# A new table of places for a two-phase Trainium2 kernel: applied-inverse sets one to a step, the inverse over four steps, its transposes behind the step of the key products, state inputs stored a step later

## The chip, the cores and the metric

The kernel runs on one core of one Trainium2 chip. The metric is the device time of one execution in microseconds. Times are given as the median of several runs.

## What is computed

The input x is (8, 1024, 256), float32: 8 sequences of the outer index, 1024 rows (tokens for the attention part, batch rows for the gated part), 256 features. Three residual layers follow each other:

```python
x = x + 0.5 * ffn(layernorm(x), ...)
x = x + attn(layernorm(x), ...)
x = x + 0.5 * ffn(layernorm(x), ...)      # the same weights as the first
```

`ffn` is a gated recurrence over the outer index (8 steps), for each row by itself:

```python
ft = sigmoid(xt @ wf.T + c @ uf.T + bf)
it = sigmoid(xt @ wi.T + c @ ui.T + bi)
gt = tanh(xt @ wc.T + c @ uc.T + bc)
c  = ft * c + it * gt
...
h = tanh(einsum('tbi,oi->tbo', x, wo) + c_final @ uo.T + bo)
```

`attn` has 16 heads of width 16. Its keys k are also its queries (a root-mean-square norm of the input by head), v is minus the static output x @ W.T, and a gated delta rule runs along the 1024 tokens:

```python
S = S * lam
err = v_t - einsum('bhk,bhkv->bhv', k_t, S)
S = S + beta * (k_t[..., :, None] * err[..., None, :])
o_t = einsum('bhk,bhkv->bhv', q_t, S)
...
return layernorm(static_out + o)
```

## The kernel before

**Blocks and steps.** The 1024 rows are cut into 8 blocks of 128. The first gated layer (`ff`) takes a block through 8 steps (one per outer index), then the second gated layer (`fg`) does the same: 16 blocks of 8 steps, numbered b = 0 to 15, i = 8b + t. A step of the gated layer is 24 weight products of 128x128 on TensorE (12 with the layer's input, 12 with the state c, `pe_step`, L471; the trace has two records for each), sigmoids and a tanh on ScalarE (L488, L495), and a product and a sum on VectorE (L515, L517) that give the next c. The end of L517 is called the cell below.

**The attention part.** The delta rule is done in chunks of 16 tokens. For a chunk a 16x16 triangular matrix is inverted, and then 64 hops (`hop_at`, two for each of 32 pieces) carry the state S along the tokens. A block n of 128 tokens passes through these named pieces:

- preparation (`prep_pe`, `prep_act`, `prep_dve`, `prep_pool`): `ln2_late` and `lc2` (statistics L83 and coefficients L89 to L95 of the layer norm), `apply` on GpSimd, `lt0`, `lt1` (transposes of the normed rows, L696), `square`, `sums` (L624), `rms` (11 operations, L57 to L65 on 128x128), `key` (L635), `keys` (L642 on VectorE, L681 on GpSimd), `v01`, `v23` (the static products, L706, copied by ScalarE at L761), `kt0`, `kt1` (transposes of the keys, L715), `km0`, `km1` (masked copies, L655, L772), `g0` to `g3` (products of keys with keys, L735; read by ScalarE at L784 and then by VectorE at L661);
- the solve (`solve_pe`, `solve_act`, `solve_dve`): `gt0`, `gt1` (transposes, L870, and the table product L805), `inv1` to `inv3` (the inversion level by level on VectorE, L821 and L824), `al`, `tt0`, `tt1` (transposes of the inverse, L882, evicted at L832 by VectorE and L853 by ScalarE), and `ta0` to `ta7` (the sets that apply the inverse to keys and values, L899; even ones are evicted by ScalarE at L860, odd ones by VectorE at L839, into `xs_out`).

The inversion has 14 levels m = 14 to 1, two operations each; L788 says which levels a piece has, and the elements of an operation are 8 x m x (15 - m):

```python
INV = {"inv1": range(C - 2, 10, -1), "inv2": range(10, 4, -1), "inv3": range(4, 0, -1)}
```

**Where a piece stands.** `PERIOD` (L159) has for each step t four lists, and `CLOSE` (L167) four lists for the end of a block. An entry (2, "tt0") at step t means: in step t of block b, do tt0 of block b - 2. Every engine walks the same table, so a place in it sets the order on TensorE, ScalarE, VectorE and GpSimd at once. `fill_table` (L197) follows it to know which use of a PSUM bank comes after which: transposes, v and al take banks 4 and 5 in turn, the g products banks 6 and 7, and set ta m bank 6 + m % 2. `refill` (L363) waits until the bank's last use has been read.

**First phase** (`first_pe`, `first_dve`, L967 to L1020, blocks 0 to 5): no hops. TensorE does half of the input products, list 0, the other half, list 1, half of the state products, list 2, the other half, list 3. VectorE and ScalarE do lists 0 to 2 before the cell and list 3 behind it.

**Second phase** (`second_pe` L1228, `second_dve` L1309, i = 48 on): hop s runs at i = 49 + s. In a step TensorE does the hop's state products (`hop_states_pe`, L1093), 8 state products of the gates, the hop's update (`hop_update_pe`, L1110), the other 4, and then four times a quarter of the next step's input products followed by one of the four lists. VectorE does in a step, in this order: zbd from the update (`state_dve`, L1134), fcig and the cell, the late normalisation (`post_dve`, L1167, L83 to L95), and all four lists. The hop's update is written to banks 4 and 5 too: `refill` for a piece in these banks waits until zbd has been read out of them on both VectorE and ScalarE (L1127), and the update waits until all pieces before it have been read. Hops and preparation overlap in blocks 6 to 9; the late normalisation runs from block 7 on.

**Transfers** go through SyncE's queue in the order of the code (`first_sp`, `second_sp`, `transfers` at L947): x1 to memory, the next x, alpha, `xs_out` in two halves (`store_xs`, L940, 512 KB twice; the eviction of the next half's sets waits for the landing), kg; in the second phase also the loads of xs and kg for hop s + 2 and the stores of e.

## Time and profile before

| | us |
|---|---|
| median of 3 runs | 1365.33 |
| lowest and highest | 1364.75 and 1370.57 |
| the profiled execution | 1362.08 |
| its span | 1360.3 |
| mean granted TensorE clock in it | 0.982 |

The span runs from the first to the last instruction of the program; the execution's own time is 1.8 us longer. The granted clock is a share of full speed: 1.00 is 2.4 GHz, 0.50 is 1.2 GHz. Busy times count each engine by itself. PE is TensorE's products, PEld its weight loads, DVE VectorE, ACT ScalarE, POOL GpSimd, SP SyncE. A timeline's row gives the start in us from the span's start, the length, the operation, and in brackets how long the engine was idle before it and what ended that; "issue" is a wait for which the profile shows no cause. A row of busy times by stretch has its start and end, its length, the busy time of PE, PEld, DVE, ACT and POOL with the records of each, the mean granted clock, the DMA engines' busy share and their GB/s.

### The profile page before, as it was taken

The numbers are of one execution on the slowest core, as the hardware profiler recorded it, in microseconds if no ns is written. First come the engines' busy times: TensorE is split into PE (matmuls) and PEld (weight loads), VectorE is DVE, ScalarE is ACT, GpSimd is POOL, SyncE is SP. The second block draws the span as 40 slices with busy tenths as digits, with TensorE's granted clock in tenths as the row PEclk, the third lists the DMA queues.
The fourth block names the chain that finished last, engine by engine and source line by source line (L and its number), as shares of the span: only waits on it lengthen the run. The fifth ranks groups of instructions, "written<-read, shape, count | busy, mean of one in ns | idle before, by whom it ended". The sixth has DMA issues, their size and how long they took to land.

```text
span 1360.3 us, 57987 instructions
## 1 busy us (share of the span) xinstructions
PE 1261.8 (93%) x25763; PEld 1167.5 (86%) x25763; DVE 856.1 (63%) x2047; ACT 665.3 (49%) x1623; POOL 273.3 (20%) x350
## 2 busy tenths in 40 slices
PE   6999999999999999898898889899999999999997
PEld 6989998989989888787778887888889989898886
DVE  4556886868778676567657764854445646354622
ACT  3344444454444545453564556356455756655432
POOL 0113112031221211112502230230230405050500
PEclk9999999999999999998899999899999999999999
DMA  4010101122121222242225213323324242333000
GB/s 147 1 63 32 66 33 67 65 79 65 52 80 51 103 70 90 69 129 71 69 65 166 66 54 112 109 83 108 117 91 147 66 134 82 110 102 109 1 32 31
DMA packets 72425, 108.35 MB, mean 80 GB/s; under 512 B 12400, under 2 KB 49520, under 8 KB 70128
## 3 DMA queue, kind: packets, MB, share of 16 engines
q1 hardware_dynamic: 72176, 104.65, 24.0%
q8 instruction: 203, 3.33, 1.0%
q14 instruction: 46, 0.38, 0.1%
HBM read 53.74 MB, written 50.86 MB: 77 GB/s over the span
## 4 chain that ended last, share of the span: by engine, by line
PE 75%; DVE 12%; ACT 7%; issue 5%; DMA 0%; SPq 0%; DVEq 0%; ACTq 0%
PE ps L471 41%; PE ps L543 7%; PE ps L899 6%; PE ps L1093 5%; PE ps L1110 4%; PE ps L706 3%; ACT gates L488 3%; ACT zbd L1127 2%; PE ps L431 2%; DVE ln_bn L83 2%; PE ps L735 1%; DVE hs L557 1%; PE ps L870 1%; PE ps L696 1%; DVE ffn_rows L568 1%
## 5 line engine op out<-in xcount | busy, mean ns | idle before, releaser
L471 PE MATMUL ps<-gates,wt 128*128 128x128 f32 x2688 | 350.5, 283 | 2.9 <-DVE gates L517 2.9
L471 PEld LDWEIGHTS ps<-gates,wt 128*128 128x128 f32 x2688 | 320.9, 195 | 14.0 <-DVE gates L517 3.6
L471 PE MATMUL ps<-ffn_rows,wt 128*128 128x128 f32 x2304 | 296.7, 281 | 10.1 <-DVE hs L557 3.7
L471 PEld LDWEIGHTS ps<-ffn_rows,wt 128*128 128x128 f32 x2304 | 276.6, 195 | 20.1 <-issue 12.5
L488 ACT ACTIVATE gates<-ps,colv 128x128 f32<-128x128 f32 x448 | 127.6, 369 | 194.8 <-PE ps L471 194.5
L515 DVE TENSOR_TENSOR fcig<-gates 128x512 f32<-128x512 f32 x112 | 83.9, 750 | 163.5 <-ACT gates L495 129.8
L1134 DVE TENSOR_TENSOR zbd<-ps,mask 64x1024 f32<-64x1024 f32 x63 | 76.5, 1214 | 127.9 <-PE ps L1110 127.9
L1196 POOL TENSOR_TENSOR ffn_rows<-ffn_rows,rowv 128x256 f32<-128x256 f32 x64 | 53.9, 878 | 347.0 <-DMA ffn_rows<-x_scratch 347.0
L1127 ACT ACTIVATE zbd<-ps,mask 32x256 f32<-32x256 f32 x252 | 103.8, 458 | 9.9 <-PE ps L1110 6.9
L899 PE MATMUL ps<-inv_cols,kv 32*32 32x32 f32 x8192 | 88.3, 194 | 15.8 <-issue 13.7
L899 PEld LDWEIGHTS ps<-inv_cols,kv 32*32 32x32 f32 x8192 | 79.1, 104 | 27.7 <-issue 18.7
L471 PE MATMUL ps<-kg_rows,wt 128*128 128x128 f32 x768 | 95.1, 278 | 6.5 <-DVE hs_more L557 3.5
L471 PEld LDWEIGHTS ps<-kg_rows,wt 128*128 128x128 f32 x768 | 89.2, 192 | 10.3 <-issue 5.8
L543 PE MATMUL ps<-wt,ffn_rows 128*128 128x256 f32 x384 | 91.8, 384 | 5.8 <-DVE hs L557 3.0
L1119 ACT COPY e<-ps 128x512 f32<-128x512 f32 x64 | 37.4, 584 | 116.2 <-PE ps L1093 116.1
L122 POOL TENSOR_SCALAR key_rows<-ffn_rows,ln_stats 128x256 f32<-128x256 f32 x64 | 40.2, 643 | 256.4 <-PE ps L870 168.1
L1093 PE MATMUL ps<-zbd,xsb 128*32 128x64 f32 x4096 | 84.1, 235 | 6.7 <-issue 6.7
L1093 PEld LDWEIGHTS ps<-zbd,xsb 128*32 128x32 f32 x4096 | 73.8, 148 | 18.0 <-issue 12.7
L543 PEld LDWEIGHTS ps<-wt,ffn_rows 128*128 128x128 f32 x384 | 70.0, 190 | 17.4 <-ACT gates L488 4.1
L681 POOL TENSOR_TENSOR kg_rows<-key_rows,g_tok 128x512 f32<-128x512 f32 x32 | 47.6, 1519 | 185.8 <-DVE key_rows L635 185.8
L83 DVE BATCH_NORM_STATS2 ln_bn<-ffn_rows 128x6 f32<-128x256 f32 x248 | 83.9, 410 | 0.5
L1110 PE MATMUL ps<-e,kgb 32*64 32x64 f32 x4032 | 74.3, 221 | 2.1 <-issue 1.1
(127 smaller groups left out, 1726.8 us busy)
## 6 DMA issues: line engine op xcount, KB each, us to landing
xs_scratch<-xs_out SPq DMA_DIRECT2D x32, 512.0 KB, 3.5
xsb<-xs_scratch SPq DMA_DIRECT2D x256, 64.0 KB
ffn_rows<-x SPq DMA_DIRECT2D x32, 256.0 KB, 3.4
x_scratch<-ffn_rows SPq DMA_DIRECT2D x32, 256.0 KB, 2.7
kg_scratch<-kg_rows SPq DMA_DIRECT2D x32, 256.0 KB, 2.8
kgb<-kg_scratch SPq DMA_DIRECT2D x256, 32.0 KB, 2.3
e_scratch<-e SPq DMA_DIRECT2D x256, 32.0 KB, 1.7
ffn_rows<-e_scratch SPq DMA_DIRECT2D x8, 1024.0 KB
```

Source lines behind the costliest of these rows:

```text
L83: link(dve.bn_stats(stats[:, b, 0:6], src[:, b, :]))
L471: mm = pe.matmul(banks[g][:, col:col + P], wt[:, w, k, m * P:(m + 1) * P], rhs, start=(x in (0, FI)), stop=(k == KT - 1 and (t == 0 or x > ...
L488: a = act.activation(gates[q][:, g, m * P:(m + 1) * P], fi[:, g * D + m * P:g * D + (m + 1) * P], ACT.Sigmoid, bias=bias[:, g, m:m + 1])
L515: dve.tensor_tensor(fcig, gates[q][:, 0:2, :], gates[q][:, 2:4, :], ALU.mult).then_inc(self.products, 2)
L543: mm = pe.matmul(h_b[j][:, e * D:(e + 1) * D], self.xnT[b.n % len(self.xnT)][:, k, 2 * j + e, :], wt[:, WO, k, :], start=(e == 0 and k == ...
L681: pool.tensor_tensor(kg_rows.rearrange("p (b h d) -> p b h d", h=H, d=HD)[:, 2 * r:2 * r + 2, :, :], key_rows.rearrange("p (b h d) -> p b ...
L899: mm = pe.matmul(dst.ps[32 * c:32 * c + 32, 32 * k:32 * k + 32], kv_of(n)[tok, lane, :], invT[tok, lane, :], start=True, stop=True, skip_g ...
L1093: mm = pe.matmul(E_BANK[32 * g:32 * g + 32, 64 * kk:64 * kk + 64], xs_cols[:, k // C, k % C, C * a:C * a + 2 * C], zbd[:, k, :], start=Tru ...
L1110: mm = pe.matmul(S_BANKS[out_rows, k % C, :], kgb[32 * g:32 * g + 32, a, 64 * kk:64 * kk + 64], es[a][32 * g:32 * g + 32, 64 * kk:64 * kk ...
L1127: act.activation(zbd[rows, C:2 * C, cols], S_BANKS[rows, :, cols], ACT.Copy, scale=mask4[rows, c:c + 1]).then_inc(z_done, 1)
L1134: dve.tensor_tensor(zbd[0:64, 0:C, :].rearrange("p k (c d) -> p k c d", c=SETS), S_BANKS[0:64, :, :].rearrange("p k (c d) -> p k c d", c=S ...
L1196: pool.tensor_tensor(xt[p][:, r, :], xt[p][:, r, :], rowv[:, 2, :], ALU.add).then_inc(post_done, 1)
```

## The change

Only numbers of the table, one split of the inversion and one line of the transfers change. By step: set ta m of a block moves so that steps 0 to 6 hold ta2, ta3, ta4, ta5, ta6 and ta7, ta0, ta1 (before: ta4; ta5 and ta6; ta7; none in step 4; ta0 and ta1; ta2; ta3 in `CLOSE`). `inv2` is cut in two (levels 10 to 8 in step 2, 7 to 5 in step 3) and the last levels, now `inv4`, move from step 3 to step 4. `v01` moves from step 3 to step 4, list 1; `v23` to the end of step 4. `sums` moves to step 3, `rms` to the end of step 4, `tt0` and `tt1` to step 5, `key` and `keys` behind them. The first half of `xs_out` is stored in step 1 in place of step 0, and behind the stores of x1.

```diff
@@ -156,15 +156,15 @@
-PERIOD = {0: ([], [(2, "g3abcd")], [], [(1, "ln2_late")]),
...
-          4: ([(1, "v23"), (1, "sums")], [(1, "rms")], [(2, "tt0")], [(2, "tt1"), (1, "key")]),
...
+PERIOD = {0: ([], [(2, "g3abcd")], [], [(1, "ln2_late"), (3, "ta2abcd")]),
...
+          4: ([(3, "ta6abcd"), (2, "inv4")], [(1, "v01")], [(3, "ta7abcd")], [(1, "v23"), (1, "rms")]),
...
-CLOSE = ([], [(2, "ta3abcd")], [], [(1, "g2abcd")])
+CLOSE = ([], [], [], [(1, "g2abcd")])
@@ -785,7 +785,7 @@
-        INV = {"inv1": range(C - 2, 10, -1), "inv2": range(10, 4, -1), "inv3": range(4, 0, -1)}
+        INV = {"inv1": range(C - 2, 10, -1), "inv2": range(10, 7, -1), "inv3": range(7, 4, -1), "inv4": range(4, 0, -1)}
@@ -947,10 +947,10 @@
-            if t in (0, 4) and stored.real:
-                store_xs(sp, stored, t // 4)
             if t in (0, 1) and prep.real:
                 store_x1(sp, prep, (2 * t, 2 * t + 1))
+            if t in (1, 4) and stored.real:
+                store_xs(sp, stored, t // 4)
```

On VectorE, block 7, the end of step 2's pieces (L821 and L824 are the two operations of a level, with the elements of each) and what follows them; before:

```order
L821 TENSOR_TENSOR prod<-inv 128x448
L824 TENSOR_TENSOR inv<-inv,prod 128x8x8x7
L821 TENSOR_TENSOR prod<-inv 128x448
L824 TENSOR_TENSOR inv<-inv,prod 128x8x7x8
L821 TENSOR_TENSOR prod<-inv 128x432
L824 TENSOR_TENSOR inv<-inv,prod 128x8x6x9
L821 TENSOR_TENSOR prod<-inv 128x400
L824 TENSOR_TENSOR inv<-inv,prod 128x8x5x10
L1134 TENSOR_TENSOR zbd<-ps,mask 64x1024
L515 TENSOR_TENSOR fcig<-gates 128x512
```

And now:

```order
L821 TENSOR_TENSOR prod<-inv 128x448
L824 TENSOR_TENSOR inv<-inv,prod 128x8x8x7
L1134 TENSOR_TENSOR zbd<-ps,mask 64x1024
L515 TENSOR_TENSOR fcig<-gates 128x512
L517 TENSOR_TENSOR gates<-fcig 128x256
L89 BN_AGGR ln_bn<-ln_bn 128x2 x8
```

Levels 7, 6 and 5 no longer stand ahead of zbd, fcig and the cell; they come after the late normalisation's coefficients of the next step.

On VectorE, block 7, from the last operation of rms on; before, in step 4:

```order
L65 SCALAR_TENSOR_TENSOR rms<-hs,rms 128x128
L832 TENSOR_SCALAR inv_cols<-ps,mask 128x128x4 x4
L635 TENSOR_TENSOR key_rows<-key_rows,rms 128x2048
L1134 TENSOR_TENSOR zbd<-ps,mask 64x1024
L515 TENSOR_TENSOR fcig<-gates 128x512
L517 TENSOR_TENSOR gates<-fcig 128x256
L642 TENSOR_TENSOR kv<-key_rows,lam_tok 128x128x16
```

And now, in steps 4 and 5:

```order
L65 SCALAR_TENSOR_TENSOR rms<-hs,rms 128x128
L1134 TENSOR_TENSOR zbd<-ps,mask 64x1024
L515 TENSOR_TENSOR fcig<-gates 128x512
L517 TENSOR_TENSOR gates<-fcig 128x256
L832 TENSOR_SCALAR inv_cols<-ps,mask 128x128x4 x4
L635 TENSOR_TENSOR key_rows<-key_rows,rms 128x2048
L642 TENSOR_TENSOR kv<-key_rows,lam_tok 128x128x16
```

The evictions of the transposed inverse (L832) and key (L635) moved behind the cell, so rms is no longer right ahead of them.

On TensorE, block 7, steps 4 and 5; before:

```order
L471 MATMUL ps<-ffn_rows,wt 128x128 x3
L706 MATMUL ps<-wt,key_cols 128x256 x8
L471 MATMUL ps<-ffn_rows,wt 128x128 x6
L882 MATMUL ps<-ident,inv 128x128 x8
L471 MATMUL ps<-ffn_rows,wt 128x128 x3
L882 MATMUL ps<-ident,inv 128x128 x8
L1093 MATMUL ps<-zbd,xsb 32x64 x32
L471 MATMUL ps<-gates,wt 128x128 x8
L1110 MATMUL ps<-e,kgb 64x64 x32
L471 MATMUL ps<-gates,wt 128x128 x4
```

And now step 4:

```order
L471 MATMUL ps<-ffn_rows,wt 128x128 x3
L899 MATMUL ps<-inv_cols,kv 32x32 x64
L471 MATMUL ps<-ffn_rows,wt 128x128 x3
L706 MATMUL ps<-wt,key_cols 128x256 x8
L471 MATMUL ps<-ffn_rows,wt 128x128 x3
L899 MATMUL ps<-inv_cols,kv 32x32 x64
L471 MATMUL ps<-ffn_rows,wt 128x128 x3
L706 MATMUL ps<-wt,key_cols 128x256 x8
L1093 MATMUL ps<-zbd,xsb 32x64 x32
```

Step 4 holds two sets and both halves of v in place of one half of v and the transposes; the transposes follow in step 5.

## Rows read from the trace of the kernel before

**Rows 1.** The page, engines: busy us (share of the span) xinstructions.

```profile
PE 1261.8 (93%) x25763; PEld 1167.5 (86%) x25763; DVE 856.1 (63%) x2047; ACT 665.3 (49%) x1623; POOL 273.3 (20%) x350
```

**Rows 2.** By stretch: its length, busy us (records) of PE, PEld, DVE, ACT, POOL; clock, DMA.

```profile
24.00:478.60 454.60, 438.08 (x7812) 412.35 (x7810) 335.40 (x858) 204.51 (x497) 86.49 (x108) 1.00 0.16 57
478.60:925.10 446.50, 403.33 (x10613) 365.29 (x10602) 300.09 (x651) 227.00 (x521) 93.95 (x116) 0.95 0.29 88
```

**Rows 3.** The same by interval: block 7 (1 to 5), block 9, one without pieces.

```profile
602.50:615.60 13.10, 13.10 (x518) 12.38 (x518) 12.09 (x38) 4.68 (x12) 4.71 (x8) 1.00 0.47 149
615.60:632.40 16.80, 12.31 (x239) 11.28 (x237) 16.35 (x29) 5.91 (x15) 7.42 (x8) 0.78 0.24 70
632.40:649.40 17.00, 16.83 (x335) 15.22 (x334) 9.23 (x33) 10.06 (x21) 1.05 (x2) 0.92 0.13 34
649.40:669.60 20.20, 16.44 (x343) 15.20 (x343) 15.45 (x21) 10.49 (x23) 17.00 (x19) 0.92 0.24 84
669.60:681.80 12.20, 11.13 (x318) 10.21 (x320) 5.32 (x6) 5.07 (x13) 0.00 (x0) 0.86 0.18 52
...
864.20:882.80 18.60, 14.47 (x438) 13.22 (x437) 18.15 (x27) 4.68 (x12) 8.46 (x8) 0.82 0.31 96
1190.90:1198.90 8.00, 8.00 (x180) 7.62 (x179) 7.24 (x15) 4.00 (x11) 0.00 (x0) 1.00 0.61 192
```

**Rows 4.** VectorE's timeline, block 7, interval 2.

```profile
621.09 0.73 DVE L839 TENSOR_SCALAR xs_out<-ps,w_x 128x512 f32<-128x512 f32 x1
...
626.39 0.62 DVE L821 TENSOR_TENSOR prod<-inv 128x448 f32<-128x448 f32 x1
...
630.09 1.21 DVE L1134 TENSOR_TENSOR zbd<-ps,mask 64x1024 f32<-64x1024 f32 x1
```

**Rows 5.** TensorE's waits, 478.6 to 1009.7 us: total, times, longest.

```profile
PE ps L899 <- issue: 13.7, 14, 3.1
PE ps L882 <- DVE inv_cols L832: 8.0, 3, 3.4
PE ps L1093 <- issue: 6.7, 5, 2.8
```

**Rows 6.** VectorE's timeline, block 7, steps 3 and 4.

```profile
635.98 0.75 DVE L839 TENSOR_SCALAR xs_out<-ps,w_x 128x512 f32<-128x512 f32 x1 [0.65 <-PE ps L899]
649.28 2.27 DVE L624 TENSOR_REDUCE rms<-key_half 128x128 f32<-128x2048 f32 x1
656.79 1.40 DVE L832 TENSOR_SCALAR inv_cols<-ps,mask 128x512 f32<-128x512 f32 x2
```

**Rows 7.** TensorE's timeline, blocks 7 to 9: the longest waits, and a half of v.

```profile
618.51 0.86 PE L899 MATMUL ps<-inv_cols,kv 32*32 32x32 f32 x48 [2.59 <-issue]
631.45 1.72 PE L696 MATMUL ps<-ident,key_rows 128*128 128x128 f32 x8 [1.91 <-DVE zbd L1134]
637.41 3.62 PE L706 MATMUL ps<-wt,key_cols 128*128 128x256 f32 x16
658.25 0.71 PE L882 MATMUL ps<-ident,inv 128*128 128x128 f32 x4 [3.40 <-DVE inv_cols L832]
871.51 1.51 PE L1093 MATMUL ps<-zbd,xsb 128*32 128x64 f32 x47 [2.83 <-issue]
```

**Rows 8.** The eleven stretches at half clock: one of them, and their sum.

```profile
631.70:635.10 3.40, 3.40 (x67) 3.17 (x69) 2.99 (x21) 2.48 (x3) 0.00 (x0) 0.50 0.09 30
...
sum 44.30, PE 42.88 PEld 39.58 DVE 28.43 ACT 11.94 POOL 24.15; mean PE 3.90 PEld 3.60 DVE 2.58 ACT 1.09 POOL 2.20
```

**Rows 9.** TensorE's waits in the first phase, 131 to 460 us.

```profile
PE ps L870 <- DVE key_rows L661: 5.7, 4, 1.4
...
PE ps L882 <- DVE inv_cols L832: 1.6, 1, 1.6
```

**Rows 10.** The page: the instruction queue, and a transfer's us to landing.

```profile
q8 instruction: 203, 3.33, 1.0%
...
xs_scratch<-xs_out SPq DMA_DIRECT2D x32, 512.0 KB, 3.5
```

10 rows, old and new, of the table PERIOD are left out of this document.

## The prediction

> **What bounds the kernel now.** I read the page's totals first, then busy times by stretch, then those of single steps, then TensorE's waits, then the timelines around the longest of them. The totals show TensorE busy for 93% of the span and VectorE for 63% [rows 1]. The change adds and removes no operation, so TensorE's 1261.8 us stay; it can only move idle time and time at half clock. By stretch [rows 2], the first phase is almost full from 24 to 478.6 us (438.08 of 454.60). From 478.6 to 925.1 us, where preparation and inverse run beside the state hops, it is busy 403.33 of 446.50 at a mean clock of 0.95. These 43 us of idle time are what the table can reach.
>
> Single intervals, from the end of one gate cell (L517) to the next, tell why. I call the one that follows the cell of step t "interval t"; VectorE does the pieces of step t in it. In block 7, VectorE is busy 12.09 of 13.10 in interval 1 and 16.35 of 16.80 in interval 2, while TensorE works 12.31 there; interval 2 of block 9 reads 18.15 of 18.60 [rows 3]. There VectorE is the bound: its zbd product (L1134), fcig and the cell stand behind all its pieces, from 630.09 to 632.4 [rows 4]. A step without pieces, the last row there, takes 8.00 with TensorE full [rows 3]. So an interval costs the larger of two sums: 8.0 plus TensorE's pieces, or VectorE's pieces plus about 2.5 for those three operations and their pauses.
>
> The other waits between 478.6 and 1009.7 us are 8.0 at the inverse's transposes (L882), which need a bank that VectorE empties only after rms, and 13.7 + 6.7 at L899 and L1093 for "issue", where the profile shows nothing that TensorE waits for [rows 5].
>
> **The inverse in four parts.** Three levels (m = 7, 6, 5) leave interval 2: six instructions, 626.39 to 630.09, 3.7 us. So does ta5's eviction (0.73), since the set left in step 2 is ta4, which ScalarE evicts [rows 4]. VectorE's pieces in intervals 1, 2 and 3 of blocks 7 and 8 become 11.4 (today's 13.1 less 2.5, plus 0.75 for ta3), 10.1 (5.5 of late normalisation from 615.6 to 621.09, and 4.6 for levels 10 to 8, between that eviction and 626.39), and 9.8 (3.0 to normalisation's coefficients, 632.4 to 635.4; sums 2.27; ta5 0.75; levels 7 to 5) [rows 3, 4, 6]. With 2.5 each this is a chain of 38.8, bound by VectorE. Interval 4 is led by TensorE: ta6, v01, ta7, v23 are 2 x 1.4 + 2 x 3.6 [rows 7], so 18.0, and 1.2 because GpSimd's work slows the cell's operations today and will again (an estimate). Sum 58.0. Today's four are 13.1 + 16.8 + 17.0 + 20.2 = 67.1, of which 3.4 is half clock on TensorE's own work (two stretches of 3.4 in intervals 3 and 4 [rows 8]): 63.7. Saving 5.7.
>
> What is late next: lt1's transposes use banks 4 and 5 and wait until VectorE has written zbd. Today they wait 1.91 [rows 7]. With ta6 no longer ahead of them I expect some 5 us of idle TensorE at that point. It lies inside the 38.8, but it shows that VectorE stays the bound for three steps.
>
> **The transposes a step later.** tt1's last four wait 3.40, because L832 stands behind sums and rms, from 649.28 to 656.79 [rows 6, 7]. In the change tt0 opens step 5, right behind the cell, and nothing is ahead of its eviction. That eviction (1.4 for a pair) still stands between tt0 and tt1's second fill, and the next one between tt1 and ta0: from the end of step 4's products that is 2.7 (to the cell's end, an estimate) + 1.4 + 0.7 + 1.4, some 6, where TensorE has about 4 us of its own work. So 2.0 are given back in step 5. key and keys (2.3 each) go to interval 5, where VectorE is busy 5.32 of 12.20 [rows 3]: hidden. **Blocks 7 and 8: -3.7 each.** Block 9 has no preparation left; its interval 2 loses the same 4.4 and interval 3 takes 1.4 of it back: **-3.** Block 6 has no late normalisation, the 5.5 that make VectorE the bound, and ln1 now stands behind key and keys: **-0.1.** Together -10.5.
>
> **First phase.** From block 2 on the largest waits are L870's 1.42 before gt0, once per block, and L882's 1.64, once [rows 9]. The latter goes: -1.6. ta2 now stands ahead of gt0 but needs g3's first bank, which VectorE frees only 0.4 before the second: 0.9 of waiting in place of 1.42, in blocks 3 to 5, -1.5. VectorE's load between two cells stays under TensorE's 11 (3.6 for v23, 2 for tt, 5.4 for the gates) in the worst step (rms, four evictions and key, 9.3, and the cell). **-3.** In the second phase ta2's bank costs 0.5 in four blocks, by the same reasoning; ta3's place between g1 and g2, whose banks it shares, becomes free, for which I take 0.75 a block: **-1.**
>
> **Stores.** The stores of xs_out go behind the x1 stores of step 1. SyncE then waits for ta3's eviction, about 5 us after the cell. Behind it stand the x1 load of blocks 7 and 8, which waits for GpSimd anyway, and the next e stores, which need the next hop. It lands 3.5 later [rows 10], ahead of ta4's eviction: 0. Without that cover ScalarE would hold the gates 1 to 3 us a block.
>
> **One set to a step.** One set is 128 products and 128 loads in 1.3 us. Of the 20.4 us of "issue", 9.8 lie in the VectorE-bound intervals (2.59 and 2.83 among them [rows 7]), 10.6 elsewhere. The longest cut a set in two where two sets stand close. The instruction queue moved 3.33 MB in 203 packets [rows 10]: 16.4 KB each, and 65 bytes for each of the 51,526 products and loads [rows 1], so a packet holds about one set. I read these waits as code that comes late. What spacing gives lies between 0 and -10.6; I take **-5**, as ta6 and ta7 still share step 4.
> The Trainium skill, "Runtime: NRT & Kernel Launch", Instruction fetch mechanics, has the same blocks of 256 instructions but calls their fetching hidden by the sequencer's pace. By it this term would be 0 and the sum 5 us higher; it speaks against what this part of the change can give.
>
> **The clock.** TensorE was granted half clock (1.2 in place of 2.4 GHz) for 44.3 us in eleven stretches, after idle time or after sets close together; 22 us at most hang on them. 17.1 us of the stretches lie in the VectorE-bound intervals, where they cost little; the rest costs up to 13.6 [rows 8]. The wait before lt1 should still bring the low level. Between 0 and -13.6; I take **-4.**
>
> **Sum.** -10.5 - 3 - 1 - 5 - 4 = -23.5 on the profiled execution of 1362.1: 1338.6. The median of the runs is 1365.3, 3.2 above it, so 1342.
>
> **Rivals.** (a) The chain moves and nothing else: neither code nor clock gains. 1365.3 - 14.5 = 1351. For it: the idle time before lt1 keeps the clock dips. Against it: sets that stop half way. It is also what the fetch rule of the Trainium skill's page gives, but for the clock.
> (b) VectorE only hands its load on. Its pieces still bind three steps, and step 4 holds 18 us of TensorE with v23 last, so that ScalarE's two copies of 0.6 and normalisation of 2.1 come ahead of the e copy: 2 to 3 more per block, and the clock dips grow with the 5 us of idle. The -14.5 shrinks to -3: 1362. For it: VectorE idles 5 us in today's interval 3, so the old table had room too. Against it: the 3.40 of L882 goes in any case.
> (c) Slower: key is late in every block. Counted from the end of step 4's products in the first phase, the cell, rms (3.6 to 4), four evictions (3.0), the pauses and key (2.3) end at about 12.2, and kt0 could start at 13.8. It decides from 1.6 us of lateness on: were key 5 us late, TensorE would idle 3.4 in each of 8 blocks, 27, less half of the gains above: +15, 1380. For it: today rms stands a step's half earlier. Against it: every term is a known duration.
>
> **How the numbers follow.** A measurement of this kernel tells about 0.5% (6.8 us) from no change. The forecast has 0.55 (1326 to 1350), (a) 0.20, (b) 0.14, (c) 0.08; 0.03 is for more than all terms at their best. At their best they are -14.5 - 10.6 - 13.6: 1326 or 1327. (b) gives 1362. Range 1326 to 1362. Faster by over 0.5% holds the forecast, (a) and the rest, 0.78; within 0.5% is (b), 0.14; slower 0.08.
>
> **What would show it.** Right: interval 2 of blocks 7 to 9 falls from 16.8 and more to about 12.6; L882 waits under 2.5 a block for L832; L696's wait for zbd grows to about 5; "issue" at L899 falls by a third or more; interval 4 reads 18 to 19. Wrong: TensorE waiting at L715 for key or at L706 for copies of v, ScalarE held at ta4 by a store's landing, or a first phase that takes longer than today's 454.6.

## The result, and the profile after

The change takes **1376.41 us** (median, 1369.77 to 1379.29) where the kernel before took 1364.75 beside it: a ratio of 1.0093, 95% interval 1.0064 to 1.0123. Ratios, here and below, leave out the few runs in a slower state of the chip, one of them at 2038.69 for the kernel before beside the change. The change is slower by about 1%, and outside the forecast range of 1326 to 1362. The profiled execution of the change took 1375.93 us with a span of 1374.1; the one of before 1362.08 and 1360.3. The sum is made between these two: +13.8.

First the page's engines, which answer to [rows 1]: the same work, TensorE 0.7 longer busy.

```profile
PE 1262.5 (92%) x25763; PEld 1169.6 (85%) x25763; DVE 862.8 (63%) x2047; ACT 666.5 (49%) x1623; POOL 272.6 (20%) x350
```

Then the change by stretch, with the borders at the same cells as in [rows 2] (478.6, 925.1), and besides these the stretch from there to the cell of step 6 of block 10. Columns: stretch, length, then busy us (records) of PE, PEld, DVE, ACT and POOL, clock, DMA share, GB/s.

```profile
24.00:478.94 454.94, 436.39 (x7544) 412.34 (x7542) 336.36 (x856) 204.09 (x494) 83.57 (x108) 0.99 0.16 54
478.94:930.06 451.12, 402.37 (x10742) 364.52 (x10730) 301.40 (x652) 227.11 (x521) 96.40 (x116) 0.96 0.29 90
930.06:1015.29 85.23, 76.77 (x2041) 70.33 (x2039) 34.68 (x67) 40.73 (x102) 17.67 (x24) 0.96 0.34 108
```

The same last stretch of the kernel before:

```profile
925.14:1001.69 76.55, 73.52 (x1913) 67.65 (x1911) 32.98 (x66) 40.18 (x101) 17.56 (x24) 0.98 0.38 121
```

So the three stretches changed by +0.3, +4.6 and +8.7 us. The numbers of records show that sets have crossed the borders, at 1.4 us each: 268 products fewer in the first stretch (ta2 and ta3 of one block now come behind it), 129 more in the second, 128 more in the third. For the same work the stretches changed by +3.1, +3.2 and +7.3, where the forecast had -3, some -20 and nothing.

The single intervals of block 7 say where the forecast was right and where it was not. In order: the interval behind step 0 (interval 0), then 1, 2, 3, 4, 5 as in [rows 3], and last interval 0 of block 8.

```profile
593.51:610.35 16.84, 12.52 (x309) 11.57 (x308) 6.95 (x17) 5.54 (x15) 0.00 (x0) 0.90 0.50 154
610.35:623.78 13.43, 13.43 (x455) 12.60 (x454) 12.43 (x39) 4.68 (x12) 4.58 (x8) 1.00 0.49 176
623.78:636.57 12.79, 7.97 (x171) 7.20 (x170) 12.55 (x20) 5.08 (x13) 7.40 (x8) 0.97 0.33 82
636.57:650.14 13.57, 13.41 (x444) 12.51 (x443) 11.69 (x33) 8.89 (x19) 1.00 (x2) 0.90 0.15 40
650.14:668.35 18.21, 17.86 (x346) 15.86 (x344) 12.28 (x25) 10.03 (x23) 11.43 (x15) 1.00 0.23 81
668.35:681.49 13.14, 11.97 (x324) 11.19 (x325) 9.76 (x10) 7.38 (x18) 6.15 (x4) 1.00 0.22 57
717.10:735.75 18.65, 13.04 (x309) 12.00 (x308) 6.94 (x17) 5.54 (x15) 0.00 (x0) 0.73 0.45 139
```

Before, interval 0 of block 7 was this:

```profile
593.73:602.47 8.74, 8.57 (x181) 7.91 (x180) 6.94 (x16) 4.84 (x14) 0.00 (x0) 1.00 0.98 319
```

Intervals 1 to 5 fell from 79.3 to 71.1. Interval 0 rose from 8.74 to 16.84, with 128 products more (ta2) that need 1.4. What it does with the other 6.7 stands in TensorE's timeline, here of the change in blocks 7 and 8 (start, us, engine, line, operation, records, and in brackets the idle time before it and what ended it):

```profile
595.17 1.79 PE L899 MATMUL ps<-inv_cols,kv 32*32 32x32 f32 x128 [0.80 <-DVE key_rows L661]
596.89 2.00 PE L1093 MATMUL ps<-zbd,xsb 128*32 128x64 f32 x64
602.18 2.07 PE L471 MATMUL ps<-gates,wt 128*128 128x128 f32 x8 [3.29 <-issue]
...
718.76 1.63 PE L899 MATMUL ps<-inv_cols,kv 32*32 32x32 f32 x128 [0.81 <-DVE key_rows L661]
720.32 0.97 PE L1093 MATMUL ps<-zbd,xsb 128*32 128x64 f32 x35
725.96 1.08 PE L1093 MATMUL ps<-zbd,xsb 128*32 128x64 f32 x29 [4.67 <-issue]
```

ta2 waits 0.8 for its bank. Behind it, after 64 and after 35 records of the hop, TensorE stops for 3.29 and 4.67 for nothing that the profile shows, and part of the interval runs at half clock (mean 0.90, 0.73). In the first phase it is the wait itself that is long. Here is the bank's wait in block 3, right behind g3's products (L735), and what VectorE did meanwhile:

```profile
218.33 1.16 PE L735 MATMUL ps<-key_half,key_cols 64*32 64x128 f32 x64
221.99 1.53 PE L899 MATMUL ps<-inv_cols,kv 32*32 32x32 f32 x128 [2.50 <-DVE key_rows L661]
```

```profile
218.84 2.71 DVE L83 BATCH_NORM_STATS2 ln_bn<-ffn_rows 128x6 f32<-128x256 f32 x8
221.47 0.86 DVE L661 SCALAR_TENSOR_TENSOR key_rows<-ps,mask,key_rows 128x256 f32<-128x256 f32 x2
```

g3's products were done at 219.49, but VectorE had 2.71 of statistics ahead of the eviction that frees the bank (L661). In the kernel before, gt0 (L870) was the first to need these evictions, and 1.60 us of input products stood between g3 and it; here in block 5:

```profile
391.64 1.60 PE L471 MATMUL ps<-ffn_rows,wt 128*128 128x128 f32 x12
394.67 1.14 PE L870 MATMUL ps<-ident,key_rows 128*128 128x128 f32 x8 [1.42 <-DVE key_rows L661]
```

In blocks 7 and 8 the order is another one: 12 records of input products (1.60 us) stand between g3 and ta2, and VectorE evicts g3 ahead of the statistics, so the wait is only 0.8. TensorE's waits over the whole span of the change, to be read beside [rows 5] and [rows 9]:

```profile
PE ps L1093 <- issue: 17.1, 13, 4.7
PE ps L899 <- DVE key_rows L661: 11.2, 6, 2.5
...
PE ps L696 <- DVE zbd L1134: 7.5, 2, 4.2
PE ps L899 <- issue: 6.1, 12, 1.7
...
PE ps L471 <- issue: 4.5, 3, 3.3
...
PE ps L882 <- DVE inv_cols L832: 1.7, 4, 0.7
```

L882's waits for L832 have fallen from 9.6 in all to 1.7 and L899's "issue" from 13.7 to 6.1. More than both has come back: at L1093 (6.7 before), at L471, and as L899's wait for g3's bank (1.3 before).

### The profile page after: what moved, and what is told of

Read it like the earlier page. It is cut to its first block, busy times and chain, and to the rows that moved or that the text cites. A ratio compares the mean times of both kernels' runs of the same rounds, so it can differ in the third digit from the quotient of the medians.

```text
span 1374.1 us, 57990 instructions
## 1 busy us (share of the span) xinstructions
PE 1262.5 (92%) x25763; PEld 1169.6 (85%) x25763; DVE 862.8 (63%) x2047; ACT 666.5 (49%) x1623; POOL 272.6 (20%) x350
## 4 chain that ended last, share of the span: by engine, by line
PE 73%; DVE 13%; ACT 8%; issue 5%; DMA 0%; SPq 0%; DVEq 0%; ACTq 0%
PE ps L471 40%; PE ps L543 7%; PE ps L899 6%; PE ps L1093 5%; PE ps L706 4%; PE ps L1110 4%; ACT gates L488 3%; ACT zbd L1127 3%; DVE ln_bn L83 2%; PE ps L431 2%; DVE hs L557 1%; DVE ffn_rows L568 1%; PE ps L696 1%; DVE fcig L515 1%; PE ps L735 1%
## 5 line engine op out<-in xcount | busy, mean ns | idle before, releaser
L471 PE MATMUL ps<-gates,wt 128*128 128x128 f32 x2688 | 351.7, 284 | 6.6 <-issue 3.9
L471 PEld LDWEIGHTS ps<-gates,wt 128*128 128x128 f32 x2688 | 322.3, 195 | 17.6 <-issue 6.1
L471 PE MATMUL ps<-ffn_rows,wt 128*128 128x128 f32 x2304 | 299.5, 282 | 10.7 <-DVE hs L557 3.7
L471 PEld LDWEIGHTS ps<-ffn_rows,wt 128*128 128x128 f32 x2304 | 278.5, 196 | 20.1 <-issue 12.6
L515 DVE TENSOR_TENSOR fcig<-gates 128x512 f32<-128x512 f32 x112 | 81.6, 729 | 146.4 <-ACT gates L495 125.3
L899 PE MATMUL ps<-inv_cols,kv 32*32 32x32 f32 x8192 | 88.5, 195 | 17.4 <-DVE key_rows L661 11.2
L899 PEld LDWEIGHTS ps<-inv_cols,kv 32*32 32x32 f32 x8192 | 80.0, 106 | 27.6 <-DVE key_rows L661 12.5
L471 PE MATMUL ps<-kg_rows,wt 128*128 128x128 f32 x768 | 95.3, 278 | 6.5 <-DVE hs_more L557 3.5
L1093 PE MATMUL ps<-zbd,xsb 128*32 128x64 f32 x4096 | 85.4, 233 | 17.1 <-issue 17.1
L1093 PEld LDWEIGHTS ps<-zbd,xsb 128*32 128x32 f32 x4096 | 74.4, 147 | 28.8 <-issue 23.9
L471 PEld LDWEIGHTS ps<-kg_rows,wt 128*128 128x128 f32 x768 | 89.2, 192 | 10.3 <-issue 5.8
```

Of the source, the lines that this page charges most:

```text
L471: mm = pe.matmul(banks[g][:, col:col + P], wt[:, w, k, m * P:(m + 1) * P], rhs, start=(x in (0, FI)), stop=(k == KT - 1 and (t == 0 or x > ...
L515: dve.tensor_tensor(fcig, gates[q][:, 0:2, :], gates[q][:, 2:4, :], ALU.mult).then_inc(self.products, 2)
L899: mm = pe.matmul(dst.ps[32 * c:32 * c + 32, 32 * k:32 * k + 32], kv_of(n)[tok, lane, :], invT[tok, lane, :], start=True, stop=True, skip_g ...
L1093: mm = pe.matmul(E_BANK[32 * g:32 * g + 32, 64 * kk:64 * kk + 64], xs_cols[:, k // C, k % C, C * a:C * a + 2 * C], zbd[:, k, :], start=Tru ...
```

## The experiments

Each ran beside the kernel before on the same chip; the ratio is to that one, with its 95% interval. They ran at several times and on several chips, where the kernel before had medians of 1363.0 to 1364.8, so microseconds of different experiments compare to 1 or 2 us at best. "Issue" below is the sum of TensorE's rows "<- issue" over the span: 24.3 us before, 31.9 in the change.

**1. ta2 alone back to where its neighbours stood.** In the change, ta2 goes from behind g3 to between g1 and g2:

```diff
-PERIOD = {0: ([], [(2, "g3abcd")], [], [(1, "ln2_late"), (3, "ta2abcd")]),
+PERIOD = {0: ([], [(2, "g3abcd")], [], [(1, "ln2_late")]),
-CLOSE = ([], [], [], [(1, "g2abcd")])
+CLOSE = ([], [(2, "ta2abcd")], [], [(1, "g2abcd")])
```

> The change, with one set put back to the end of the block: ta2 stands in CLOSE instead of at the end of step 0. Theory A (the site of ta2): in the profile of the change the interval from the cell of step 0 to that of step 1 is 6 to 10 us longer than before in blocks 7 to 10 and 2 to 5 us in blocks 3 to 5, of which 1.4 is the set's own work; all of it but the 1.4 goes, some 30 us, so the time is 1344 to 1352, faster than before by 1 to 1.5%. Theory B (the cost is the transposes of the inverse and key in step 5, whose intervals grew by 2.5 in step 5 and 1 to 3 in step 6 of each block): the intervals of steps 5 and 6 stay as long as in the change and the time stays within 8 us of it, 1368 to 1376.

Measured: 1350.15, ratio 0.9912 (0.9876 to 0.9948): 26 us faster than the change. The first row is its first phase, the second its second, the third interval 0 of block 7:

```profile
24.00:473.90 449.90, 434.58 (x7677) 409.41 (x7675) 336.17 (x856) 204.97 (x495) 83.51 (x108) 1.00 0.16 55
473.90:905.24 431.34, 395.02 (x10614) 356.16 (x10602) 300.94 (x653) 226.44 (x520) 96.57 (x116) 0.98 0.30 94
589.57:598.32 8.75, 8.58 (x181) 8.04 (x180) 6.93 (x16) 4.84 (x14) 0.00 (x0) 1.00 0.75 234
```

Everything else of the change is worth -4.7 in the first phase, of which 1.4 is ta3's crossing of the border, so -3.3, and -15.2 in the second. In the stretch behind it, to step 6 of block 10, it costs +4.9 (81.46 in place of 76.55). The whole loss hangs on the place of one set of eight. Cell by cell, interval 0 of blocks 3 to 10 is 42.6 us longer in the change than here, and the block ends, which no longer hold the set, are 14.6 shorter: 28.0 of the 28.7 between the two spans.

**2. Sets alone, 3. VectorE's pieces alone.** Experiment 2 has the change's sets, v and stores with VectorE's pieces as before (inverse in three parts, tt in step 4); experiment 3 the other way round, with ta1 and ta2 in step 6. Only the lines on step 4 are shown.

```diff
 # 2, against the change
-          4: ([(3, "ta6abcd"), (2, "inv4")], [(1, "v01")], [(3, "ta7abcd")], [(1, "v23"), (1, "rms")]),
+          4: ([(3, "ta6abcd"), (1, "sums")], [(1, "rms"), (1, "v01")], [(3, "ta7abcd"), (2, "tt0")], [(2, "tt1"), (1, "key"), (1, "v23")]),
 # 3, against the kernel before
-          4: ([(1, "v23"), (1, "sums")], [(1, "rms")], [(2, "tt0")], [(2, "tt1"), (1, "key")]),
+          4: ([(1, "v23"), (2, "inv4")], [], [], [(1, "rms")]),
```

> The sets, v01, v23 and the stores in the places of the change; the inverse (three parts), sums, rms, tt, key and keys where they were before. Theory A: the long interval 0 of the change is there in full (14 to 19 us in blocks 7 to 9), and without the relief of VectorE in steps 2 to 4 the time is above the change's: 1382 to 1395. Theory B: without the late transposes the loss is gone, 1360 to 1368.

> The inverse over four steps, sums, rms, tt, key and keys where the change has them; ta3 to ta7, v01, v23 and the stores where they were before, ta1 and ta2 in step 6 (ta1 can't stand in step 5 before the transposes are out). Theory A: interval 0 is as short as before (8.7 us in block 7) and intervals 2 to 4 are as short as in the change, so 1348 to 1358. Theory B: the late transposes cost here what they cost in the change: 1368 to 1380.

Measured: 2 takes 1396.8 (1.0252, 1.0207 to 1.0298), 2 us above its range, 3 takes 1383.3 (1.0145, 1.0093 to 1.0197). In 2, block 7's interval 2 is still bound by VectorE (16.17 of 16.62), and interval 4 has both loads, two sets and v as well as sums, rms and tt:

```profile
638.02:654.64 16.62, 8.05 (x171) 7.27 (x170) 16.17 (x27) 5.08 (x13) 7.55 (x8) 0.80 0.21 63
670.10:693.10 23.00, 20.95 (x448) 18.71 (x448) 15.75 (x22) 11.48 (x25) 12.19 (x17) 1.00 0.20 68
```

Experiment 3 was expected at 1348 to 1358 and missed by 25. In its waits the transposes of the inverse stand out. tt stands a step later, and v23, which stands right ahead of it in the change, does not cover it here:

```profile
PE ps L882 <- DVE zbd L1134: 12.2, 3, 5.0
PE ps L882 <- DVE inv_cols L832: 11.2, 5, 2.7
```

So the parts of the change are not additive. VectorE's pieces alone lose 1.4%, and together with the sets and v (without ta2's place) they gain 13 us. Experiment 2 has ta2 in its dear place too: taking off the 26 us of experiment 1 gives some 1371, an estimate that no run shows. That it is v in the gap ahead of tt that makes VectorE's part pay is read from the waits; no run moves v alone.

**4. A small load of e.** The 1 MB load that fills the DMA engines when ta2 runs is cut to 128 of its 2048 columns.

```diff
-                    sp.dma_start(xn_flat, e_d[n % 2]).then_inc(y_in, 16)
+                    sp.dma_start(xn_flat[:, 0:P], e_d[n % 2][:, 0:P]).then_inc(y_in, 16)
```

> The change, but the load of e in step 1 (1 MB, eight times) brings only its first 128 of 2048 columns; the rest of the late normalisation's input is left over from before. Theory C (in step 0 and 1 the code of TensorE comes late because its 16 KB packets stand behind that load: in the profile of the change one comes 8.2 us after the one before it, and TensorE stops for 3.3 to 4.7 us with no wait shown): these stops in interval 0 of blocks 7 to 10 fall below 1 us each and the time falls by 10 to 15 us, 1362 to 1367. Theory D (they come late because g3, ta2 and the hop follow each other too densely, whatever else is on the queues): the stops stay at 3 to 5 us and the time within 3 us of the change's.

Measured: 1368.7 (1.0046, 1.0023 to 1.0068), 7.7 less than the change, between the two theories. The stop behind ta2 in block 7 is 1.93 in place of 3.29: the load makes it longer, but the stop is there without it.

```profile
599.87 3.78 PE L471 MATMUL ps<-gates,wt 128*128 128x128 f32 x16 [1.93 <-issue]
```

**5. ta2 ahead of g3**, so that its bank is free sooner:

```diff
-PERIOD = {0: ([], [(2, "g3abcd")], [], [(1, "ln2_late"), (3, "ta2abcd")]),
+PERIOD = {0: ([(3, "ta2abcd")], [(2, "g3abcd")], [], [(1, "ln2_late")]),
```

> The change, with the set ta2 ahead of g3 in step 0 in place of right behind it: the number of instructions in the step is the same, only the order of ta2 and g3 on their shared banks changes. Theory A1 (the wait for g3's eviction is what brings the stops and the half clock: the set waits 2.5 us in the first phase and 0.8 to 2.0 in the second): the waits of L899 for key_rows vanish, the interval behind step 0 falls back to what it was before plus 1.4 for the set, and the time is 1349 to 1356. Theory A2 (it is the place itself: one set more in the step that has g3, and in the second phase a hop, with instruction code that comes late): the waits go, but the stops of 3 to 5 us and half clock in blocks 7 to 10 stay, and the time is 1366 to 1374, some 5 to 8 below the change.

Measured: 1360.41 (0.9987, 0.9962 to 1.0012), again between. The bank's wait was worth a part: from the last cell of block 2 to that of block 5 the kernel is 5.5 shorter, though ta2 still waits 1.1 a block there. In block 7 the stop stays though ta2 waits for no bank:

```profile
599.30 2.58 PE L471 MATMUL ps<-gates,wt 128*128 128x128 f32 x16 [3.40 <-issue]
```

**6. The stores alone**, on the kernel before:

```diff
-            if t in (0, 4) and stored.real:
+            if t in (1, 4) and stored.real:
```

(behind the x1 stores, as in the change).

> The kernel before, with nothing but the stores of xs_out moved as in the change (behind step 1's x1 stores, and behind nothing else in step 4). The prediction put this part at 0: expected within 3 us of the kernel before. If the stores matter through ScalarE (an eviction that waits for their landing) or through the e load behind them, it is 3 us or more off, 1367 to 1385.

Measured: 1382.57 (1.0149, 1.0107 to 1.0191). ScalarE's waits have a new row, for ta4's eviction, which needs the store's landing:

```profile
ACT xs_out L860 <- DMA xs_scratch<-xs_out: 73.8, 8, 10.6
```

The expectation (within 3 us) missed: in the kernel before ta4 stands in step 1 itself, so the edit takes away the cover that the prediction had named. In the change ta4 stands a step behind the store, and this row is absent, which bears out the term of 0. Without the cover the later store costs 18 us, 2.3 a block, where the prediction had 1 to 3.

**7. One more set in the step that VectorE bounds, 8. the inverse in three parts**, both against experiment 1 (of 7 the line on step 2 is shown; ta6 moves to step 3 too, so that step 4 has ta7 alone):

```diff
 # 7
-          2: ([], [(3, "ta4abcd")], [], [(1, "lt0"), (2, "inv2")]),
+          2: ([(3, "ta4abcd")], [], [(3, "ta5abcd")], [(1, "lt0"), (2, "inv2")]),
 # 8
-        INV = {..., "inv2": range(10, 7, -1), "inv3": range(7, 4, -1), "inv4": range(4, 0, -1)}
+        INV = {..., "inv2": range(10, 4, -1), "inv3": range(4, 0, -1)}
```

> The version with ta2 between g1 and g2 (1350), and besides ta5 moved into step 2, ta6 into step 3 and ta7 alone in step 4, so that one set fills part of the 4.8 us in which TensorE waits for zbd ahead of lt1, and step 4, which TensorE bounds, has one set less. If VectorE bounds interval 2 and TensorE interval 4: interval 2 grows by 0.75 (ta5's eviction), interval 4 falls by 1.4, half clock ahead of lt1 goes: 1343 to 1349. If instruction code that comes late decides, two sets in step 2 bring a stop there in some blocks and nothing is gained: 1350 to 1356.

> The version with ta2 between g1 and g2 (1350), with the inverse's levels in three parts as before (10 to 5 in step 2, 4 to 1 in step 3); all else as there. The prediction's chain says that three levels (3.7 us) return to interval 2, which VectorE bounds, and leave interval 3 one level more and interval 4 four fewer: interval 2 is 16.5 again, interval 3 grows little, the later steps stay, so +3.7 in blocks 7, 8 and 9 each and 11 in all: 1358 to 1363. The rival says that VectorE only hands its load on and the partition is worth little: 1348 to 1353.

Measured: 7 takes 1351.63 (0.9914, 0.9882 to 0.9946), 8 takes 1362.74 (0.9989, 0.9966 to 1.0011). 8 is 12.6 above experiment 1 (11 forecast). Interval 2, the one that the chain names, is 3.8, 3.8 and 4.3 longer in blocks 7, 8 and 9 than in experiment 1, 12.0 together. Here it is for block 7:

```profile
612.00:628.62 16.62, 7.71 (x169) 6.93 (x167) 16.17 (x27) 5.07 (x13) 7.47 (x8) 0.79 0.24 64
```

So the cut of the inverse is worth about what the whole version gains, in this setting; in experiment 3 the same cut did not pay. In 7, the second set of step 2 stopped half way, though TensorE had 4.8 us to spare there, and half clock came with it. Interval 4 did fall, from 17.9 to 17.0, so the two cancelled:

```profile
618.81 0.86 PE L899 MATMUL ps<-inv_cols,kv 32*32 32x32 f32 x48 [2.41 <-issue]
```

**What the stops have in common.** The stops put down to "issue" show no cause, so I looked at where in the program they stand. I numbered all of TensorE's records of a trace in order of time: loads, products and its semaphore instructions (which the rows leave out). In the kernel before, 15 of the 16 stops of over 0.4 us put down to "issue" come ahead of a record whose number is 193 or 194 modulo 256; in the change 22 of 22, in experiment 1 21 of 23. The packets of the instruction queue (q8, 16 KB each, one for some 256 records) tell the rest. Here is the DMA view of the change for block 7's stop, first of the 6.8 us ahead of a packet, then of the 2.4 us behind its start:

```profile
q1 hardware_dynamic: 563, 1.65, 78.1%
ffn_rows<-e_scratch SPq DMA_DIRECT2D x1, 1024.0 KB, 6.1
```

```profile
q1 hardware_dynamic: 117, 0.10, 17.6%
q8 instruction: 1, 0.02, 2.5%
```

From 593.0 to 599.8 no code packet moved, while the engines were 78% busy (the e load, 6.1 to its landing). One started at 599.9, and TensorE went on at 602.18. In block 8 the same: none from 715.8 to 723.6 at 72.9%, one at 723.7, on at 725.96. Theory F: code comes by blocks; a block run faster than the next one comes makes TensorE stop at its border. A set is 256 instructions in 1.3 us, one whole block if it is aligned so.

The traces let this be followed border by border. Each trace has 203 such packets and 203 or 204 places 193 modulo 256, and the packets pair with the places in order. At not one of these places, in sixteen traces, did TensorE go on less than 2.15 us after the packet of that place had started. In the median a packet starts 0.9 us after TensorE has passed the border before, in every trace between 0.8 and 0.9. Behind the border just ahead of the stop in block 7 it started 4.14 us later in the change and 1.04 later in experiment 4, where the load is small; in block 8, 4.61 and 1.06. So the packets come about one block ahead of TensorE, and with the 1 MB load on its way these two started some 3 us later.

**9, 10, 11. Shifting the code.** Tiny products ahead of TensorE's first one move every later instruction by 64 or 144 places. 9 is the kernel before, 10 is experiment 1, both by 64; 11 is the change by 144, with 36 of these products.

```diff
             pe.wait_ge(v_in, 32)
+            for _ in range(16):
+                pe.matmul(ps[7][0:2, 0:1], colv[:, 3, 0:2], colv[:, 3, 0:1], start=True, stop=True)
+            pe.wait_ge(u_in, 16 * 3)
```

> The kernel before with 16 tiny products (64 instructions of TensorE: each product is two loads and two products in the profile) ahead of its first one, in the 7 us in which TensorE waits for its first weights. Nothing else is different, but every later instruction of TensorE sits 64 places further on. Theory F (code comes in blocks of 256 instructions, and a block that is run faster than the next one comes makes TensorE stop at the border; in the traces of before, of the change and of the version with ta2 between g1 and g2 every stop of over 0.4 us put down to issue lies at place 193 or 194 of 256 in the order of loads and products): the stops move to other places (64 instructions earlier in the program), the first phase, which had none before 478 us, gets some 10 us of them, the total of issue rises from 25 to 35 to 45 us, and the time is 1372 to 1392. Rival G (the stops hang on what the instructions are and on semaphores, not on their places): same stops, 1361 to 1368.

> The version with ta2 between g1 and g2 (1350), with the same 64 instructions ahead of everything. Theory F: 10 us or more of stops appear in the first phase, issue in all from 26 to 36 to 48 us, and the time is 1358 to 1378. Rival G: 1348 to 1353.

> The change with 36 tiny products (144 instructions) ahead of everything; they take about 15 us from 3 us on, so some 8 us are added at the start, which are not of interest. Theory F: the stops of 3.29 and 4.67 us in the interval behind step 0 of blocks 7 and 8 vanish (the set ta2 no longer fills one block of code), those intervals take 10 to 12 us in place of 16.8 and 18.6, while the first phase gets some 10 us of stops it does not have: 1375 to 1395 in all. Rival G, or the theory that the set's place is dear at any alignment: the intervals keep their stops, 1382 to 1388.

Measured: 9 takes 1380.07 (1.0126, 1.0086 to 1.0167): **16 us for an edit that changes no work and no order.** Its first phase, from 24 us to the same cell, is 465.60 long in place of 454.60, and has stops that the kernel before has not. Issue is 30.3 in all, a rise of 6 where theory F expected 10 or more:

```profile
24.00:489.60 465.60, 444.21 (x7806) 417.98 (x7805) 335.00 (x857) 205.13 (x496) 86.24 (x108) 0.99 0.16 55
```

```profile
PE ps L899 <- issue: 3.6, 3, 1.4
PE ps L471 <- issue: 3.1, 3, 1.6
```

10 takes 1352.18 (0.9918, 0.9886 to 0.9949), level with experiment 1 within the noise, where theory F expected 8 us more or above. Its count of stops was too high for that kernel (issue 24.6, none in the first phase). The time is that of rival G, but the stops themselves moved to other places of the program. 11 takes 1379.27 (1.0121, 1.0080 to 1.0162). Its intervals 0 of blocks 7 and 8, same order, same bank wait, same e load:

```profile
603.30:614.88 11.58, 10.36 (x310) 9.47 (x309) 6.95 (x16) 5.51 (x15) 0.00 (x0) 1.00 0.54 159
723.00:734.89 11.89, 10.17 (x309) 9.39 (x308) 6.94 (x17) 5.56 (x15) 0.00 (x0) 1.00 0.52 166
```

The two intervals take 11.6 and 11.9 in place of 16.8 and 18.7, as forecast by F. The total did not fall: other borders took the gain back (issue 35.7 in all), and the start took 1.9. In the three experiments every stop over 0.4 but two is again at number 193 or 194, that is at other places of the program.

**12, 13, 14. Halving the sets**, so that none fills a block. 13 halves ta2 in the change, 12 the sets ta0, ta1 and ta3 to ta7 of experiment 1, 14 only ta4, ta6 and ta0 of it.

```diff
 # 13, against the change
-PERIOD = {0: ([], [(2, "g3abcd")], [], [(1, "ln2_late"), (3, "ta2abcd")]),
-          1: ([(2, "gt0")], ...
+PERIOD = {0: ([], [(2, "g3abcd")], [], [(1, "ln2_late"), (3, "ta2ab")]),
+          1: ([(3, "ta2cd"), (2, "gt0")], ...
 # 12 and 14, against experiment 1, the lines on ta4
-          2: ([], [(3, "ta4abcd")], [], [(1, "lt0"), (2, "inv2")]),
-          3: ([(1, "lt1"), (1, "square")], ...
+          2: ([], [], [], [(3, "ta4ab"), (1, "lt0"), (2, "inv2")]),
+          3: ([(3, "ta4cd"), (1, "lt1"), (1, "square")], ...
```

> The version with ta2 between g1 and g2 (1350), with the sets ta0 and ta3 to ta7 in halves of 128 instructions, the halves in different places, where possible in different steps with a hop's products between them (ta3 in steps 1 and 2, ta4 in 2 and 3, ta0 in 5 and 6; ta1, ta5, ta6 and ta7 in two places of one step); the stores of xs_out stand in steps 2 and 4. Theory F (TensorE stops at a border of 256 instructions where it ran the block before it in less than the 3.5 us that the next one takes to come): no block is run in 1.3 to 2 us any more, the total of issue falls from 26 to under 13, and the time by half of that and the half clock that follows: 1338 to 1346. Rival G (the stops hang on something else near the sets): issue stays at 20 to 30, 1347 to 1355.

> The change with ta2 alone in halves: the first where ta2 stands in the change, the second in step 1 ahead of gt0, behind the hop's products; the wait for g3's bank is still there (2.5 us in the first phase, 0.8 to 2 in the second). Theory F: the stops of 3.29, 4.67 and 3 us in the interval behind step 0 of blocks 7, 8 and 10 vanish with most of their half clock, those intervals take 10 to 12.5 us in place of 16.8, 18.7 and 14.3, and the time is 1357 to 1366. Rival G: stops as in the change, 1372 to 1380.

> The version with ta2 between g1 and g2 (1350), with only ta4, ta6 and ta0 in halves, each pair of halves in neighbouring steps with a hop's products between (ta4 in steps 2 and 3, ta6 in 3 and 4, ta0 in 5 and 6), and the stores of xs_out where that version has them, so that no eviction waits for a store's landing (e12 had 5.1 us of that on ScalarE in blocks 3 to 5) and no half of v waits for ta7. Theory F: issue falls from 26 to 18 to 22, the first phase keeps its time, 1342 to 1348. Rival: the halves cost elsewhere what they save, 1349 to 1356.

Measured: 13 takes 1367.07 (1.0014, 0.9980 to 1.0048), 9 less than the change and 1 above what F expected. F had the stops vanish; they got shorter and moved behind the hop's update, to 2.40 in block 7 (3.29 in the change) and 1.73 in block 8 (4.67):

```profile
612.14 0.50 PE L1110 MATMUL ps<-e,kgb 32*64 32x64 f32 x17 [2.40 <-issue]
```

12 takes 1368.21 (1.0025, 0.9997 to 1.0053), a miss: issue fell to 19.9, but its own store of xs_out in step 2 stood right ahead of ta4's eviction:

```profile
ACT xs_out L860 <- DMA xs_scratch<-xs_out: 21.6, 6, 5.1
```

14 mends that and takes 1353.52 (0.9929, 0.9908 to 0.9951): issue 22.8, nothing gained over experiment 1, a miss for F's forecast of 1342 to 1348. Fewer instructions at once shortened the stops of experiment 13 where they were; which other bursts then meet a border was not under control. **Experiment 1 remains the fastest version**; 7, 10 and 14 can't be told from it.

## Why the prediction was wrong

**The chain was right where it mattered, and exact by luck.** Interval 2 was to be 12.6 and is 12.79; L882's waits were to be under 2.5 a block and are 0.7 at most; L696's wait for zbd was to be about 5 and is 4.2; interval 4 was to be 18 to 19 and is 18.21. Intervals 1 to 4 of block 7 sum to 58.00, the forecast 58.0, but from errors that cancel: 13.9, 12.6, 12.3 and 19.2 were worked out, 13.43, 12.79, 13.57 and 18.21 came. Interval 3 was not bound by VectorE (11.69 busy) but by TensorE (13.41 of 13.57, at a mean clock of 0.90), and the 1.2 for GpSimd in interval 4 did not come: the cell's two operations (L515 and L517), 1.10 and 1.16 us long there before and 0.69 and 0.42 where GpSimd is idle, took 0.80 and 0.42. Experiment 8 puts the inverse in four parts at 12.0 in interval 2 of three blocks (forecast 3 x 3.7). "First phase: -3" measured -3.3 without ta2's place (experiment 1), and no wait for the stores' landing appears under the cover named.

**The step that failed** is on ta2: "ta2 now stands ahead of gt0 but needs g3's first bank, which VectorE frees only 0.4 before the second: 0.9 of waiting in place of 1.42", and "in the second phase ta2's bank costs 0.5 in four blocks". It has two errors. The first is the wait in the first phase. The 1.42 that gt0 waited were left over after 1.60 of input products, and ta2 follows g3 with nothing between: 1.42 + 1.60 - 0.4 = 2.6, where the prediction had 0.9. Measured are 2.50 in each of blocks 3 to 5, and half clock followed in two of them. In the second phase the waits are 0.8 in blocks 7 and 8 and 2.0 in block 9, 3.6 in all for a forecast of 2.0. The second error is larger: the place was priced by its waits alone. A set's 128 loads and 128 products close behind g3's records and ahead of a hop's came with stops of 3.29, 4.67 and 3.0 in blocks 7, 8 and 10, which the prediction's sum has nowhere. Together the place costs 26 us, by experiment 1. Experiments 5 and 13 change the wait and the set's size and each win part of it back (16 and 9); experiment 11 moves the code and takes 12 out of two intervals, though not out of the total.

**One set to a step: -5** was read from the right cause and priced with the wrong rule. I took the stops for code that comes late, which experiments 9 and 11 and the packets bear out; but I took spacing as the remedy. What matters too is which 256 instructions share a block, and every move reshuffles that for all behind it: issue went from 24.3 to 31.9, in experiment 1 to 25.3, so the term was about +1 there and +8 in the change, and not -5.

The rule of the Trainium skill, "Runtime: NRT & Kernel Launch", Instruction fetch mechanics, that fetching is hidden by the sequencer's pace, would have given 0. The runs disagree with it for bursts of small products (stops of up to 4.67), and agree with the blocks of 256 instructions that the same section gives (321 of 338 stops over sixteen traces at number 193 or 194 of 256).

**The clock: -4** did not come. The mean clock fell from 0.982 to 0.980: a stretch at half clock counts half, so about 1374.1 x 0.020 x 2 = 55 us were at 1.2 GHz against 1360.3 x 0.018 x 2 = 49. The 6 us more cost 3 at most, so the term was between 0 and +3. In experiment 1's profile the clock is 0.991, 24 us at the low level, so 25 less and up to 12 gained; but that is one of its two best runs (0.985 to 0.991 over seven, the kernel before 0.979 to 0.987 beside them), and what the term is worth there stays rough. In the change the low level came behind idle time of TensorE (2.50 in blocks 3 and 4, the stops in 7 and 8).

**Block 10** was not in the sum and gave +7.3 for the same work. Its interval 0 has ta2 and a stop, and is 6.1 longer. Its interval 4 has two sets and is 4.9 longer, more than the 3.8 that interval 2 gave back. In experiment 1, without ta2's place, the stretch is still 4.9 longer than before.

**Block 9: -3** came in part. Its interval 2 fell by 5.7, from 18.60 to the following, and intervals 3 to 6 took 4.0 of it back, where the forecast had 1.4; over intervals 1 to 6 it is -1.7. In experiment 1 interval 2 fell by 5.1, 3.3 came back, and it is -1.8:

```profile
870.83:883.73 12.90, 11.09 (x404) 10.21 (x404) 12.32 (x20) 4.68 (x12) 5.71 (x7) 1.00 0.46 143
```

The rivals: (c), slower by a late key, named the right side but not the mechanism; no row waits for key at L715 in the change. (a), the chain alone, is nearest to what experiment 1 shows (1351 forecast, 1350.15 measured). That is partly luck: the second phase gave 15.2 where (a) had 11.5, clock and code included, and the stretch behind it took 4.9 that no rival had.

## What to carry to other kernels

Price the place of a burst of small TensorE instructions by what stands directly ahead of it in both queues, by the bank it reuses, and by the code it brings. A wait for a bank counts from the eviction's place in the evicting engine's own order, and the work that has covered it so far has to be added when the new place lacks that cover. After any reordering look at the rows "<- issue" first: if stops stand at one place modulo 256, some of the gain or loss belongs to how the code falls into blocks and not to the schedule, and a shift of the whole program by some instructions gives an idea of how much (here 2 to 16 us). Undo the parts of a table one at a time: here one bad place outweighed all the good ones.

## What the runs showed of the hardware

TensorE stopped at fixed places of its instruction stream: 321 of the 338 stops of over 0.4 us in sixteen traces come at number 193 or 194 of 256, and it went on 2.1 to 3.4 us after the code packet in front of the stop had started. Two such packets were never seen to start less than 3.2 us apart; a set runs its 256 instructions in 1.3. When the DMA engines were 73 to 78% busy with the 1 MB load, the packet started 4.14 and 4.61 us behind the border in place of 1.04 and 1.06 with the small load, and block 7's stop was 3.29 in place of 1.93. Whether the packet waits in a queue behind the load's own packets or for something else that the load holds is not in the trace. That 64 instructions in idle time cost the kernel before 16 us and another version of it 2, within the noise, was not expected either: how much a shift does can't be read from one kernel for another, and my count of borders by instruction numbers overrated it for experiment 10.

Open: why half clock came in some blocks behind the same wait and not in others (0.88 and 0.77 in blocks 3 and 4, 1.00 in block 5, all with 2.50 of waiting), and a placement that keeps all sets off the borders, which was not found in experiments 12 and 14. Of the 16 us in experiment 9, 11 are in the first phase, where the stops sum to 6.7; how the rest splits between half clock and the other blocks was not followed.
